# An output projection as three rounded passes, and a context bank turned sooner and divided later

## What is computed

```
ctx = einsum('bhqk,bhkd->bhqd', attn, v)      # softmax(q k^T / sqrt(8)) v
attn_out = ctx @ wo.T + bo
x = layernorm(x + attn_out, ln1_g, ln1_b)
```

## Time and profile before

| what | value |
|---|---|
| median of 3 runs | 1558.99 us |
| profiled execution | 1559.22 us |
| its span | 1557.5 us |
| outside the span | 1.7 us |
| mean granted TensorE clock | 0.982 of full |
| busy PE, DVE, ACT, POOL | 96%, 75%, 72%, 65% |

### The profile page before, as it was taken

One profiled execution on the slowest core, in us unless ns is written; L12 is line 12 of the kernel. 1 busy time (PEld: TensorE's weight loads), 2 busy tenths in 40 slices (PEclk: granted clock), 3 DMA queues, 4 the chain that ended last, 5 costly groups with the idle time before them and its releaser, 6 DMA issues.

```text
span 1557.5 us, 26116 instructions
## 1 busy us (share of the span) xinstructions
PE 1502.6 (96%) x8318; PEld 832.5 (53%) x8318; DVE 1160.8 (75%) x1834; ACT 1121.3 (72%) x1636; POOL 1014.9 (65%) x978
## 2 busy tenths in 40 slices
PE   4888999999999999999999999999999999999997
PEld 3433555555555555555555555555555555555476
DVE  3767677878778787777877778777777777767486
ACT  2466777677776777777677777777777777777776
POOL 3521668767686776868767686776757677667343
PEclk7799999999999999999999999999999999999999
DMA  7433333152332514233142331514323251521111
GB/s 177 119 92 86 96 87 85 49 140 53 81 91 56 130 42 105 74 88 91 49 131 61 81 92 45 141 48 116 83 75 98 69 117 43 142 51 36 41 43 33
DMA packets 75309, 130.06 MB, mean 84 GB/s; under 512 B 10613, under 2 KB 39206, under 8 KB 70566
## 3 DMA queue, kind: packets, MB, share of 16 engines
q1 hardware_dynamic: 73894, 124.19, 31.2%
q0 software_dynamic: 1280, 4.20, 1.0%
HBM read 97.42 MB, written 29.62 MB: 82 GB/s over the span
## 4 chain that ended last, share of the span: by engine, by line
PE 84%; DVE 8%; issue 3%; SPq 1%; DMA 1%; ACT 1%; POOL 1%; DVEq 0%; ACTq 0%; POOLq 0%
PE hid_y L1013 16%; PE ctx_ps L1208 14%; PE hid_y L1017 13%; PE hid_y L1014 13%; PE score L1056 12%; DVE negmax L881 3%; PE misc L1013 2%; PE score L1076 1%; PE misc L1148 1%; DVE x1n L349 1%; PE score L1013 1%; PE misc L1105 1%; PE misc L1164 1%; PE misc L1141 1%; PE misc L1014 1%
## 5 line engine op out<-in xcount | busy, mean ns | idle before, releaser
L881 DVE TENSOR_REDUCE negmax<-score 128x2 f32<-128x1024 f32 x484 | 590.5, 1220 | 239.4 <-PE score L1056 239.4
L592 POOL TENSOR_TENSOR hidl<-hid,hidh 128x512 fp32r<-128x512 f32 x456 | 584.4, 1293 | 258.1 <-DVE hidh L838 140.8
L711 ACT ACTIVATE probs<-score 128x1024 f32<-128x1024 f32 x468 | 479.5, 1024 | 108.7 <-PE score L1076 108.5
L740 ACT ACTIVATE hid<-hid_y,cols 128x512 f32<-128x512 f32 x484 | 330.9, 684 | 161.9 <-PE hid_y L1017 154.2
L1208 PE MATMUL ctx_ps<-probs,V 128*18 128x512 f32 x2048 | 271.5, 602 | 3.2 <-DVE ctxT L888 3.2
L1056 PE MATMUL score<-Kp,Qp 24*128 24x512 f32 x968 | 244.9, 500 | 23.8 <-DMA Kp<-k_parts_dram 16.1
L1076 PE MATMUL score<-Qp,Kp 32*128 32x512 f32 (+1 forms) x1024 | 265.9, 499 | 0.0
L1013 PE MATMUL hid_y<-x1h,w1h 128*128 128x512 f32 x484 | 236.2, 488 | 1.5 <-DVE negmax L881 1.3
L369 POOL TENSOR_TENSOR yacc<-yacc,gated 128x512 f32<-128x512 f32 x127 | 170.6, 1343 | 61.8 <-DVE gated L854 61.8
L737 ACT ACTIVATE hidh<-hid_y,cols 128x512 fp32r<-128x512 f32 x256 | 174.7, 682 | 34.4 <-PE hid_y L1017 31.9
L1056 PEld LDWEIGHTS score<-Kp,Qp 24*128 24x128 f32 x968 | 90.5, 183 | 197.4 <-issue 138.2
(11 more groups left out here) (203 smaller groups left out, 1828.4 us busy)
## 6 DMA issues: line engine op xcount, KB each, us to landing
gate_b<-gate_dram SPq DMA_DIRECT2D x128, 256.0 KB, 3.6
q_parts_dram<-q_parts SPq DMA_DIRECT2D x48, 256.0 KB, 3.0
k_parts_dram<-k_parts SPq DMA_DIRECT2D x48, 256.0 KB, 3.1
Qp<-q_parts_dram SPq DMA_DIRECT2D x64, 192.0 KB
Kp<-k_parts_dram SPq DMA_DIRECT2D x64, 192.0 KB
Qp<-q_parts_dram SPq DMA_DIRECT2D x30, 240.0 KB
Kp<-k_parts_dram SPq DMA_DIRECT2D x30, 240.0 KB
Qp<-q_parts_dram SPq DMA_DIRECT2D x30, 144.0 KB
```

The lines of the kernel that those rows point to most:

```text
L592: pool.tensor_tensor(hidl[:, n % RING, :], hid[:, n % 2, :], hidh[:, n % RING, :].bitcast(F32), ALU.subtract).then_inc(s["h_lo"], 1)
L711: act.activation(probs[:, n % 2, 2 * j:2 * j + 2, :], score2[:], ACT.Exp, scale=SCALE)\
L740: act.activation(hid[:, n % 2, :], hid_bank(u, n), ACT.Relu, bias=col(n))\
L881: dve.tensor_reduce(negmax[:, g % 2, :, k % 8], banks_for_max(u.count(32, k))[:], AX.X, ALU.max, negate=True).then_inc(s["a_max"], 1)
```

## The change

The product x1 becomes `three` on rounded parts. At set-up DVE makes `woh` (a rounded copy of `woT`) and `wol` (the rest). Per unit ACT makes `ctxh`, a rounded copy of `ctxT` (**x1c**, tick 27.5), and DVE makes `ctxl`, the rest (**x1d**, tick 28: behind the gate product of unit `i-2` and ahead of the reduction of unit `i`). The two live in the tiles `ch` and `cl`. PE's first pass waits for `c_ch`, its third for `c_cl`. The transpose of ctx0 moves to `T = 58.5`; its reciprocal and its division move to **ctx0n**, `T = 60.5`. ctx1 is as before in its order.

```diff
-    "f_k": -23, ..., "ctx0": 59.5,
-    "ctx1": 89, "cT": 90.5, "x1": 93.5, "x1p": 92.5, ...
+    "f_k": -23, ..., "ctx0": 58.5, "ctx0n": 60.5,
+    "ctx1": 89, "ctx1n": 89, "cT": 90.5, "x1c": 91.5, "x1d": 92, "x1": 93.5, "x1p": 92.5, ...
@@
+        woh, wol = sb("woh", [128, D], F32R), sb("wol", [128, D], F32R)
+        ctxh, ctxl = ch[:], cl[:]
@@ ScalarE
                 if T == u.at["f_ch"]:
                     wait(act, s["f_conv"], u.count(1, 1))
                     wait(act, s["f_qk"], u.count(2, 0))
+                    wait(act, s["c_x1"], u.n - 1)
                     act.activation(ch[:], misc[:], ACT.Identity, bias=col(V_CONV)).then_inc(s["f_ch"], 1)
...
+                if T == u.at["x1c"]:
+                    wait(act, s["c_cT"], u.count(1, 1))
+                    wait(act, s["f_qk"], 2 * min(u.n + 2, UNITS))
+                    act.activation(ctxh, ctxT[:], ACT.Copy).then_inc(s["c_ch"], 1)
@@ VectorE, set-up
+                dve.wait_ge(s["set_wo"], 1)
+                dve.tensor_copy(woh[:], woT[:]).then_inc(s["set_wo"], 1)
+                dve.wait_ge(s["set_wo"], 2)
+                dve.tensor_tensor(wol[:], woT[:], woh[:].bitcast(F32), ALU.subtract).then_inc(s["set_wo"], 1)
@@ VectorE
                     dve.transpose(ctxT[:], ctx_ps[:]).then_inc(s["a_ctx"], 1)
-
+                if T in (u.at["ctx0n"], u.at["ctx1n"]):
+                    g = int(T == u.at["ctx1n"])
                     sums = ctxT[:]...
...
+                if T == u.at["x1d"]:
+                    wait(dve, s["c_ch"], u.count(1, 1))
+                    dve.tensor_tensor(ctxl, ctxT[:], ctxh.bitcast(F32), ALU.subtract).then_inc(s["c_cl"], 1)
                 if T == u.at["x1p"]:
@@ TensorE
-                    wait(pe, s["c_cT"], u.count(1, 1))
-                    pe.matmul(misc[:], woT[:], ctxT[:], start=True, stop=True).then_inc(s["c_x1"], 1)
+                    wait(pe, s["c_ch"], u.count(1, 1))
+                    wait(pe, s["set_wo"], 3)
+                    three(misc[:], woh[:], wol[:], ctxh, ctxl, before_rlo=(s["c_cl"], u.count(1, 1)))\
+                        .then_inc(s["c_x1"], 1)
```

## The result

The median went from 1558.6 us (1557.2 to 1561.3, 4 runs) to 1573.6 us (1571.9 to 1574.3, 4 runs): ratio 1.0093, 95% interval 1.0076 to 1.0110. The change makes the kernel slower by 15 us. The profiled execution took 1571.85 us with a span of 1570.0, against 1559.22 and 1557.5: 12.5 us more span, at a mean granted clock of 0.981 (before 0.982). The three other executions of the changed kernel have spans of 1571.3 to 1572.5 at a mean clock of 0.978 to 0.979, so a part of the remaining 2.5 us may be the clock's; they were not traced, and that part stays open.

What follows compares the result with a forecast made beforehand. The prediction took PE's in-order stream, busy for 96% of the span, as the bound. It summed +11.9 us for x1 and -1 for ctx0 to +10.9, forecasting 1570 us, range 1561 to 1580.

Steps and rivals of the forecast that it cites:

- Pass 3 waits on x1d: In x1, PE's third pass waits for DVE's x1d about 16 times, 0.7 to 0.8 us each.
- Price per unit: x1's delay of the next expert product: +0.76 us in a unit with mid, +0.67 without.
- The hand-over: In x1, 0.15 us from the end of x1d on DVE to the start of PE's pass 3.
- The DVE operation ends behind POOL's: x1d, falling into POOL's L592 on SBUF tiles, ends only after it: 859.0 + 0.55 = 859.55.
- Three passes save 0.16: x1 in three passes takes 1.04 us for 1.20; with operands in time, 0.16 us saved per unit, 2.6 in all.
- ACT's stop: x1c holds ACT ahead of block 22's eviction; alone it would stall PE's next expert product by 0.3 us.
- The last unit: Last unit's x1: x1d beside POOL's addition delays pass 3, moving the mark from 1483.48 to 1484.8: +1.3 us.
- rival C: ACT's stop makes pass 1 of x1 wait too, 1.3 us in all units: 1580; chance 0.10.
- ctx0 at 0 a unit and -1 in all: ctx0's earlier turn gains what its division takes back: 0 per steady unit, -1 us in all, mostly the last unit's.
- Rival A: x1's parts are in time for pass 3; passes save 2.6 us, the turn up to 3.2: 1553; chance 0.10.
- Rival B: x1's stall is absorbed to 0.2 us a unit by hidden slack, the turn keeps 3.2: 1559; chance 0.12.

Runs made afterwards that it cites:

- no_x1d: Changed kernel with the old ctx0 and without x1d; the third pass multiplies by the rounded part again: 1558.1 us, ratio 0.9999.
- load_only: Changed kernel with the old ctx0 and float32 x1; x1c and x1d still made and waited for, but read by no product: 1560.0 us, ratio 1.0013.
- x1d_first: Changed kernel with the old ctx0 and x1d half a tick sooner, ahead of `f_xl` and the gate product: 1589.2 us, ratio 1.0211.
- late_own0: Changed kernel with x1 two ticks later in units 1 to 14 only, mid's steps moved, ctx0 transpose at 58.5, division at 62.5: 1561.7 us, ratio 1.0025.
- turn_div62: Changed kernel with float32 x1, no rounded parts per unit, and ctx0's division at tick 62.5 instead of 60.5: 1557.1 us, ratio 0.9994.
- turn_alone: Changed kernel with float32 x1 and no x1c or x1d, keeping the moved ctx0 turn and division: 1561.0 us, ratio 1.0024.
- three_alone: Changed kernel with the three passes kept but ctx0 turned and divided at tick 59.5 as before: 1570.6 us, ratio 1.0079.
- late_x1m: Changed kernel with the old ctx0, x1 and its followers two ticks later in all units, mid's two steps moved: 1564.9 us, ratio 1.0041.
- parts_div62: Changed kernel, three passes included, with ctx0's division at tick 62.5 instead of 60.5: 1567.9 us, ratio 1.0060.
- old_last: Changed kernel with the old ctx0 (turn and division at tick 59.5) in unit 15 alone: 1572.9 us, ratio 1.0097.

## Why the prediction was right, and where not

The forecast was 1570 with 1561 to 1580, slower with 0.78; the median is 1573.6, and the mechanism is the one named: pass 3 waits for x1d, which stands behind the gate product and ends behind POOL's operation, in every unit but unit 0, and nothing gives it back. The sum is nearer than its parts: in the profiled execution x1 costs 10.9 in all (9.2 + 0.6 + 1.1) for the 11.9 forecast, ctx0 1.7 (1.4 + 0.3) for -1, the half clock 1.5 and the tail 0.3 for nothing, and the start gives back 1.8. Of the 15.0 between the medians 2.5 are not accounted for. The change cost 4.1 us more than the +10.9 forecast: ctx0 (2.7 over), the clock (1.5), the tail and these 2.5 add to it, x1 (1.0 under) and the start (1.8) take from it. That the sum came so near is in part luck.

- **Pass 3 waits on x1d: right.** 15 waits, 0.6 at most. I had 0.7 to 0.8 each. `no_x1d` and `load_only` together show that x1d's lateness is the cause: the loss goes when x1d goes, and all but 0.08 to 0.15 of it goes when x1d stays but PE does not wait for it.
- **Price per unit: right in kind, 0.05 to 0.1 too high.** 0.71 with mid for 0.76, 0.57 without for 0.67. x1d ends 1.24 behind the start of pass 1 (864.32 - 863.08), where I had 1.25; but pass 3 starts 0.05 after that, not 0.15, and 0.57 from there to the mark is as forecast. The hand-over was mis-sized: I had it from a transpose to a small matmul. (The forecast's own figures, 860.27 - 859.50 and 1133.10 - 1132.42, give 0.77 and 0.68 where it says 0.76 and 0.67.) An iteration with mid grows by 0.85 with ctx0's share, not by 0.7 to 0.8.
- **The DVE operation ends behind POOL's: right.** Here x1d started 0.19 before the end of POOL's first L594, took 0.74 (0.68 alone) and ended 0.55 behind it, as forecast. `x1d_first` shows the full price when it falls into one early: 1.52.
- **Three passes save 0.16: right, but nowhere cashed.** 1.04 against 1.20 stood again in `late_own0`. In x1's old place it goes to ACT's stop; two ticks later, without mid, it goes (argued, not shown) to the transposes.
- **ACT's stop, "a stall of 0.3 by itself": too dear.** `no_x1d`: 0.19 with mid and less without. In the change the expert product stands behind x1d and does not wait for the eviction again, as forecast. L744 behind x1c starts 0.41 ahead of pass 1, where L737 started 1.82 ahead of x1: 1.4 later for the 1.5 forecast.
- **The last unit: 1.3 forecast, 1.1 measured, by another way.** I had x1d beside POOL. In fact x1d took its plain 0.68; PE started x1 0.61 later in its stream (0.90 after the start of the matmul ahead of it, where before it was 0.29). The profile names no releaser for this wait; x1c ends at 1493.92, 0.10 before pass 1, which points to x1c. This is rival C's condition, met in this one unit. Pass 3 cost the other 0.5.
- **ctx0 at 0 a unit and -1 in all: wrong.** It costs 0.11 an iteration (13 of them: +1.4), the edge I gave as +0.10, and 0.3 in the last hand-over where I expected -0.7. The waits for the bank went as forecast, the cast took 1.32 (0.42 usually) and ended 0.28 behind POOL, and the division took 0.81 for the expected 0.8. The mis-sized piece is this last one: the reduction of tick 62 starts as soon as the division ends, and the scores behind it wait. `turn_div62` shows that the division's place is the cause: with the division out of that gap the turn's gain stays, 0.10 an iteration. In the times, `turn_alone` is 2.9 above the kernel before beside it and `turn_div62` 0.6 below.
- **Not in the sum at all: the clock.** 1.5 us behind the last hand-over, and the first reduction, 1.6 sooner, the other way. Each is larger than the error of x1's sum (1.0) and smaller than that of ctx0's (2.7).

The Trainium skill (SBUF — State Buffer, Who interferes with whom) has a VectorE operation with two SBUF inputs contend with a GpSimd operation that reads SBUF, and says that a cast can contend when it runs in a mode that takes both port pairs; the second to come is blocked whole. The rows agree that both kinds are held up: x1d took 1.52 for 0.68, the cast 1.32 for 0.42. They end 0.55 and 0.28 after POOL's operation, which is less than their own 0.68 and 0.42, so by the recorded spans they are not blocked to its very end; here the measurement decides.

Rival A (parts in time, 1553) needed a free place. Of the two places tried, the one ahead of `f_xl` meets POOL in units 1 to 14. The later one meets it in full with mid; without mid it does so for less (0.85 for 0.68), and there the parts are in time, but the rounds still cost 0.11 more than before. Rival B (absorbed) fell: the loss per unit is uniform. Rival C (1580) held in the last unit alone.

## What to carry to other kernels

Splitting an operand for a cheaper product adds work to two other engines just before the product; price the arrival of the last part against PE's turn before counting the saved passes. Put a DVE operation with two SBUF inputs where POOL is idle, and look at what shares its bank or stands behind it: 0.68 us of work cost 0.6 to 0.7 in one place and 1.7 in another. A step split off an earlier one needs a gap of its own; the same division cost 0.2 us an iteration in one round and nothing in the next.

## What the runs showed of the hardware that I had not expected

- x1d ends 0.55 us behind the end of the POOL operation in which it starts, to 0.01 us, in units 1 to 14 of all eight kernels that have x1d (the change, `three_alone`, `load_only`, `x1d_first`, `late_x1m`, `late_own0`, `parts_div62`, `old_last`), whether it takes 0.73, 0.85, 1.34 or 1.51. So its end can be forecast from POOL's alone.
- Behind the last hand-over the granted clock fell to 0.66 of full over 5 us (3.4 us of them at 1.2 instead of 2.4 GHz, matmuls of 0.39 taking 0.63) in the change and in `turn_alone`, both with a wait of PE of 1.72, and in `parts_div62` with one of 1.31. It stayed at full in the nine others, with waits of 1.31 and 1.32, the kernel before among them. A longer wait goes with the fall but isn't needed for it; what decides is open.
- Such a stretch of 3.4 us costs 1.4 to 1.5 us: 1.5 behind the change's last hand-over, 1.4 and 1.5 in iterations 3 and 14 of `x1d_first` against their neighbours. The kernel before has one at 144 us; the kernels without it there (`three_alone`, for one) gain 1.4 in that place.
- In iteration 1, where PE has gaps in any case, the granted clock between 116 and 140 us was 1.00 (before, the change), 0.93 (`turn_alone`, `late_own0`), 0.86 (`x1d_first`) and 0.79 (`late_x1m`); x1's rounds of that iteration cost 0.6 (the change), 1.5, 1.8, 2.7 and 4.2 us. Small differences early in a run are not those of the steady state.
- Four 128x128 transposes took 0.41 us to the start of a product with 128 stationary columns (before, 1223.37 to 1223.78) and 0.58 to that of one with 18 (`late_own0`, 1224.89 to 1225.47).
